# Attention inside a feed-forward sandwich: both layer norms of a batch in one ScalarE pass, whole-batch transfers in four pieces, V copied by VectorE, maxima placed either side of the scores

## The chip, the cores and the metric

One core of one Trainium2 chip runs the whole kernel. The metric is the device time in microseconds, the median of several runs; lower is better. Engines are named as in the profile: PE is TensorE (PEld its weight loads), DVE is VectorE, ACT is ScalarE, POOL is GpSimd, SP issues all DMAs.

## What is computed

Eight batches of 1024 tokens and 256 features go through half a mixture-of-experts feed-forward (`f1`), an attention (`at`), and the same feed-forward again (`f2`). Each stage gets a layer norm of its input, and the attention normalises once more inside:

```python
x = x + 0.5 * ffn(layernorm(x))
x = x + attention(layernorm(x))        # attention adds its own input as residual
x = x + 0.5 * ffn(layernorm(x))

def attention(x):                      # x is layernorm(x) already
    h = (x - mean) * rsqrt(var + 1e-5) * ln_scale + ln_bias
    c_q, c_kv = h @ w_down_q.T, h @ w_down_kv.T
    q, k, v = up-projections to 16 heads of 64; rotary embedding on q and k
    attn = softmax(q @ k.T / 8)
    return (attn @ v) @ w_out.T + x
```

So the residual of the attention stage is x + layernorm(x), and the down-projections read layernorm(layernorm(x)). The change touches the attention alone.

## The kernel before, in words

Three stages run one after the other: `ffn("f1")`, `attention`, `ffn("f2")`. In each, one list `order` of steps, written by rules, sets the order of every engine: `tensor`, `scalar`, `vector`, `gpsimd` and `sync` walk the same list and take the steps that concern them. Engines meet through semaphores only, and each works its own queue strictly in order.

The attention has NN = 64 "heads" n: step n is a pair of heads of one batch (8 batches, 8 pairs). A head has 8 **periods**, numbered 0 to 7 here. In a period PE does

- two score tiles (L827): for a key tile of 128 keys, 2 heads x 512 queries, three products with float32 values split in a high and a low part, added onto a PSUM buffer that ScalarE has *filled* beforehand with the negated row maxima (L913, from `SH`);
- two maxima matmuls for the next head (L806, step `most`), whose result VectorE reduces to row maxima (L988);
- two attend steps (L838): the exponentials `PT` times V;
- and, in `OT`, one or two of the small products: `raise` (q or k of the next head, L785), `value` (V, L797), `row` (the maxima transposed, L813), `sum` (L849), `outward` (the output projection, L862, at the odd heads' periods 0, 3 and 4), `turn` and `latent` (once per batch).

ScalarE does the exponentials (L922), the fills of the next period's two score tiles, and copies out of PSUM: `raise` (L890), `high` (L896, two per head, both in period 0), `value` (L901), `row`, `sum`, `attend`. VectorE does the two maxima reductions and then, late in the period, the rotary product (L971, reads PSUM), the rotation sum (L978, `rotate`, periods 4 to 7), `qlow` (L983), the residual addition (L1009), the sum of two row-sum halves (L997) and its reciprocal. GpSimd adds up the exponentials (L1053, `gather`), multiplies by the sines (L1032), divides, and makes `KL`.

The rows of maxima go over SP through memory: `row` is copied to `ML`, written to `MD` (L1081), and read back onto all partitions as `SH` (L1087, `shift`); ScalarE's fills wait for that.

Score tiles and maxima share a ring of three PSUM buffers, handed out in the order in which the steps stand: a use waits until the use three places earlier is read out.

```python
ring = Banks(3, [s for s in order if s[0] in ("score", "most")])
...
order += begin.get(g, []) + scores + mosts + early.get(g, []) + fills + attends
order += [("gather",) + s[1:] for s in attends if s[3] % 4] + late.get(g, []) + end.get(g, [])
```

At a batch boundary the batch `b + 2` is loaded by one 1 MB DMA (L1058), behind the store of batch b (L1114) for which it waits; both stand in SP's queue. In the next two heads the layer norms of the following batch run in two rounds r over 17 periods: 8 statistics (L948), 8 aggregates (L954) and 8 normalisations (L960, 128x256 each) on VectorE, the power -0.5 on GpSimd (L1020, L1022), and in the second round GpSimd's addition of the first norm onto X (L1026).

## Time and profile before

| | us |
|---|---|
| runs (3) | 4356.98, 4357.19, 4368.64; median 4357.19 |
| the profiled execution's own time | 4368.48 |
| its span | 4366.7 |
| PE busy | 4005.4 (92%) |
| ScalarE, GpSimd busy | 3010.3 (69%), 3049.4 (70%) |
| VectorE busy | 2756.6 (63%) |

Busy shares are means over three stages; the first exponential of the attention starts at 615 us, the last pair at 3800 us. Matmuls are pipelined and overlap in the records, so that PE's busy time is not PE at its peak. A timeline row merges like instructions that follow each other (xN).

### The profile page before, as it was taken

The numbers are of one execution on the slowest core, as the hardware profiler recorded it, in microseconds if no ns is written. First come the engines' busy times: TensorE is split into PE (matmuls) and PEld (weight loads), VectorE is DVE, ScalarE is ACT, GpSimd is POOL, SyncE is SP. The second block draws the span as 40 slices with busy tenths as digits, with TensorE's granted clock in tenths as the row PEclk, the third lists the DMA queues.
The fourth block names the chain that finished last, engine by engine and source line by source line (L and its number), as shares of the span: only waits on it lengthen the run. The fifth ranks groups of instructions, "written<-read, shape, count | busy, mean of one in ns | idle before, by whom it ended". The sixth has DMA issues, their size and how long they took to land. (4 is left out here: it accounts for less than half of the span.)

```text
span 4366.7 us, 65862 instructions
## 1 busy us (share of the span) xinstructions
PE 4005.4 (92%) x24896; PEld 2256.7 (52%) x24896; DVE 2756.6 (63%) x3555; ACT 3010.3 (69%) x3800; POOL 3049.4 (70%) x1597
## 2 busy tenths in 40 slices
PE   7999869999899989999998999899889999879999
PEld 6888724444344434444444444344444444358888
DVE  5556457656766675766667666766776667345653
ACT  4454348787778777877887787788777887735444
POOL 3444438878778787878887788788877887724444
PEclk9999979999999999999999999999999999979999
DMA  3333221111111211121112112111211121123332
GB/s 109 100 117 107 79 77 52 50 57 61 62 57 54 69 50 57 55 78 53 50 60 69 52 62 69 49 50 59 71 52 59 50 79 52 41 92 117 117 100 66
DMA packets 193645, 301.12 MB, mean 69 GB/s; under 512 B 50766, under 2 KB 101680, under 8 KB 192688
## 3 DMA queue, kind: packets, MB, share of 16 engines
q1 hardware_dynamic: 193328, 296.92, 21.2%
q8 instruction: 196, 3.21, 0.3%
q14 instruction: 121, 0.99, 0.1%
HBM read 201.92 MB, written 26.74 MB: 52 GB/s over the span
## 5 line engine op out<-in xcount | busy, mean ns | idle before, releaser
L988 DVE TENSOR_REDUCE atNM<-atPS 128x2 f32<-128x1024 f32 x1024 | 1205.9, 1220 | 804.0 <-PE atPS L806 801.4
L1053 POOL TENSOR_TENSOR atACC<-atACC,atPT 128x1024 f32<-128x1024 f32 x512 | 1285.1, 2510 | 63.0 <-ACT atPT L922 10.3
L922 ACT ACTIVATE atPT<-atPS 128x1024 f32<-128x1024 f32 x1024 | 995.7, 1023 | 201.7 <-PE atPS L827 195.1
L913 ACT ACTIVATE atPS<-atSH 128x1024 f32<-128x1024 f32 x1024 | 1009.5, 1022 | 87.1 <-DVE atNM L988 45.0
L838 PE MATMUL atPO<-atPT,atV 128*64 128x512 f32 x4096 | 974.3, 596 | 0.0
L1053 POOL TENSOR_TENSOR atACC<-atPT 128x1024 f32<-128x1024 f32 x256 | 624.0, 2437 | 105.3 <-PE atOT L849 103.7
L1032 POOL TENSOR_TENSOR atVT<-atVT,atSIN 128x512 f32<-128x512 f32 x256 | 342.8, 1339 | 366.6 <-DMA atVT<-atR 366.5
L806 PE MATMUL atPS<-atKH,atQH 64*128 64x512 f32 x2048 | 465.1, 455 | 121.0 <-ACT atPT L922 95.1
L838 PEld LDWEIGHTS atPO<-atPT,atV 128*64 128x64 f32 x4096 | 281.2, 137 | 477.1 <-issue 470.4
L827 PE MATMUL atPS<-atQH,atKL 64*128 64x512 f32 x2048 | 476.9, 462 | 45.2 <-ACT atPS L913 45.2
L827 PE MATMUL atPS<-atQH,atKH 64*128 64x512 f32 x2048 | 413.4, 399 | 0.0
L827 PE MATMUL atPS<-atQL,atKH 64*128 64x512 f32 x2048 | 412.7, 399 | 0.0
L827 PEld LDWEIGHTS atPS<-atQH,atKL 64*128 64x128 f32 x2048 | 195.1, 187 | 395.9 <-ACT atPS L913 208.5
L978 DVE TENSOR_TENSOR atU<-atU,atVT 128x512 f32<-128x512 f32 x256 | 393.0, 1535 | 3.4 <-POOL atVT L1032 3.4
L806 PEld LDWEIGHTS atPS<-atKH,atQH 64*128 64x128 f32 x2048 | 198.5, 189 | 368.1 <-ACT atPT L922 300.6
L506 POOL TENSOR_TENSOR f2GL<-f2GF,f2GH 128x512 fp32r<-128x512 f32 x144 | 199.6, 1389 | 257.8 <-ACT f2GH L354 253.1
L506 POOL TENSOR_TENSOR f1GL<-f1GF,f1GH 128x512 fp32r<-128x512 f32 x144 | 198.3, 1381 | 255.3 <-ACT f1GH L354 253.7
L890 ACT ACTIVATE atR<-atOT 128x512 f32<-128x512 f32 x256 | 153.1, 598 | 190.2 <-PE atOT L785 190.2
L862 PE MATMUL atOT<-atWO,atAT 128*64 128x256 f32 x2048 | 248.5, 385 | 19.2 <-POOL atAT L1038 13.4
L1038 POOL TENSOR_TENSOR atAT<-atAT,atRSUM 128x512 f32<-128x512 f32 x128 | 161.4, 1282 | 100.8 <-DMA atRSUM<-atRD 100.7
L827 PEld LDWEIGHTS atPS<-atQH,atKH 64*128 64x128 f32 x2048 | 197.9, 189 | 46.3
L862 PEld LDWEIGHTS atOT<-atWO,atAT 128*64 128x64 f32 x2048 | 143.7, 138 | 144.0 <-issue 41.4
(238 smaller groups left out, 6593.2 us busy)
## 6 DMA issues: line engine op xcount, KB each, us to landing
atVT<-atR SPq DMA_DIRECT2D x512, 128.0 KB, 2.0
atSH<-atMD SPq DMA_DIRECT2D x128, 512.0 KB, 4.4
f1GB<-f1GD SPq DMA_DIRECT2D x128, 256.0 KB, 6.8
atRSUM<-atRD SPq DMA_DIRECT2D x128, 256.0 KB, 4.0
f2GB<-f2GD SPq DMA_DIRECT2D x128, 256.0 KB, 6.9
x<-X SPq DMA_DIRECT2D x7, 1024.0 KB, 4.8
X<-x SPq DMA_DIRECT2D x7, 1024.0 KB, 5.4
f1XB<-in_x SPq DMA_DIRECT2D x5, 1024.0 KB, 5.3
```

The lines of the kernel that those rows point to most:

```text
L506: pool.eng.tensor_tensor(GL[n % NH][:, :], GF32[n % NH][:, :], GH[n % NH][:, :], ALU.subtract).then_inc(low_h.sem)
L806: ins = pe.eng.matmul(bank[:, h, :], QH[n % 2][HI[h], q * 128:(q + 1) * 128], KH[n % 2][HI[h], t * 512:(t + 1) * 512], start=True, stop=True)
L827: ins = pe.eng.matmul(bank[:, h, :], kk[HI[h], keys], q[HI[h], sl], start=False, stop=k == 2, skip_group_check=True)
L838: ins = pe.eng.matmul(PO[HI[h], :], V[n % 2][:, j, HI[h]], PT[k % NPT][:, h, :], start=j == 0, stop=j == T - 1)
L862: ins = pe.eng.matmul(OT[HI[c], i * D:(i + 1) * D], AT[:, (n - GP + 1 + q) % NAT, tok:tok + 64], WO[:, (p - GP + 1 + q) * D:(p - GP + 2 + ...
L913: act.eng.activation(PS[ring.of[("score", n, t, j)]][:, :, :], SH[t][:, :, :], ACT.Copy).then_inc(filled[j % 2].sem)
L922: act.eng.activation(PT[k % NPT][:, :, :], PS[ring.of[step]][:, :, :], ACT.Exp, scale=SCALE).then_inc(grown.sem)
L978: dve.eng.tensor_tensor(U[:, i, sl], U[:, i, sl], VT[k][:, :], ALU.add).then_inc(rotated.sem)
L988: dve.eng.tensor_reduce(NM[:, q // 4, :, q % 4, t], PS[ring.of[step]][:, :, :], AX.X, ALU.max, negate=True).then_inc(most_out.sem)
L1032: pool.eng.tensor_tensor(VT[k][:, :], VT[k][:, :], SIN[:, t * 512:(t + 1) * 512], ALU.mult).then_inc(sined.sem)
L1038: pool.eng.tensor_tensor(o, o, RSUM[n % 2][:, t * 512:(t + 1) * 512], ALU.mult).then_inc(divided.sem)
L1053: pool.eng.tensor_tensor(total[:, :, :], begun[:, :, :], PT[k % NPT][:, :, :], ALU.add).then_inc(gathered.sem)
```

## The change

In words, by steps:

- The list of a period becomes first maxima, two score tiles, second maxima, instead of scores, then both maxima.
- Step `value` (the copy of V out of PSUM) moves from ScalarE to VectorE, in the same place of the list.
- The row-sum halves are added by a reduction of one operand into a new `RI`, not by an addition of two.
- A batch's statistics are taken once, of X. GpSimd works out from mean and variance a scale and a bias for layernorm(layernorm(x)) and another pair for x + layernorm(x) (11 small dependent instructions); ScalarE applies both, 16 activations of 128x256 in four steps `norm`. The normalisations on VectorE, the second statistics and GpSimd's large addition go.
- Store and load of a batch become four DMAs of 256 KB each, each with its own semaphore and its own place in the list.

```diff
@@ the list @@
-                        again = [s and (s[0], b, r, s[1]) for r in range(2) for s in once()]
-                        for i, step in enumerate(again):
-                            at(end, m, -42 + i * 17 // len(again), *([step] if step else []))
+                        for i in range(4):
+                            at(end, m, -40 + i, ("stats", b, i))
+                            at(end, m, -33 + i, ("norm", b, i))
+                        at(end, m, -36, ("spread", b))
...
+                if p == NP - 1:
+                    for u, period in enumerate((25, 26, 28, 30)):
+                        at(end, m, period, ("store", b, u))
+                        if b + 2 < NB:
+                            at(end, m, period + 3 - u // 2, ("load", b + 2, u))
...
-                order += begin.get(g, []) + scores + mosts + early.get(g, []) + fills + attends
+                order += begin.get(g, []) + mosts[:1] + scores + mosts[1:] + early.get(g, []) + fills + attends
@@ scalar @@
+                    if name == "norm":
+                        _, b, i = step
+                        X = X0 if b == NB else XB[b % 2]
+                        act.wait_ge(*scales(b, 10 if b < NB else 3))
+                        act.wait_ge(*turned(b - 1, 1, 1))
+                        for k in (2 * i, 2 * i + 1):
+                            one, two = (slice(x * T + k, x * T + k + 1) for x in range(2))
+                            ins = act.eng.activation(Y[:, k, :], X[:, k, :], ACT.Identity, scale=A[:, two], bias=B[:, two])
+                            if b < NB:
+                                ins = act.eng.activation(X[:, k, :], X[:, k, :], ACT.Identity, scale=A[:, one], bias=B[:, one])
...
@@ vector @@
+                    elif name == "spread":
+                        _, b = step
+                        dve.wait_ge(*stats(b))
+                        dve.wait_ge(*scales.past(b - 1, 10))
...
+                    elif name == "value":
+                        _, n, t = step
+                        dve.wait_ge(*valued(n, t))
+                        dve.wait_ge(*attended.past(n - 2, 1, T - 1))
+                        dve.eng.tensor_copy(V[n % 2][:, 4 * t:4 * t + 4, :],
+                                            OT[:, :].rearrange("p (i d) -> p i d", d=128)).then_inc(value_out.sem)
...
-                        dve.eng.tensor_tensor(RQ[:, 0, :], RQ[:, 0, :], RQ[:, 1, :], ALU.add).then_inc(inverse.sem)
+                        dve.wait_ge(*lines.past(n - 1))
+                        dve.eng.tensor_reduce(RI[:, :], RQ[:, :, :].rearrange("p h i -> p i h"), AX.X, ALU.add,
+                                              negate=False).then_inc(inverse.sem)
@@ gpsimd, each of these waits for the one before @@
+                        then(0, pool.eng.tensor_scalar(RS[:, :], var, EPS, None, ALU.add))
+                        then(1, pool.eng.tensor_tensor(RS[:, :], RS[:, :], HALF[:, :], ALU.pow))
+                        then(2, pool.eng.tensor_scalar(NG[:, :], mean, -1.0, None, ALU.mult))
...
+                            then(8, pool.eng.tensor_tensor(A[:, two], A[:, two], HALF[:, :], ALU.pow))
+                            then(9, pool.eng.tensor_tensor(A[:, two], A[:, two], RS[:, :], ALU.mult))
+                            then(10, pool.eng.tensor_tensor(B[:, two], A[:, two], NG[:, :], ALU.mult))
@@ sync @@
-                def load(b):
-                    sp.wait_ge(*stored[b % 2].past(b - 2))
-                    sp.eng.dma_start(XB[b % 2][:, :, :], rows(src, b)).then_inc(loaded[b % 2].sem, 16)
+                def load(b, u):
+                    some = slice(2 * u, 2 * u + 2)
+                    sp.wait_ge(*stored[u].past(b - 2))
+                    sp.eng.dma_start(XB[b % 2][:, some, :], rows(src, b)[:, some, :]).then_inc(loaded[u].sem, 16)
```

PE, one period in the middle of a head (`atPS` with `atKH,atQH` alone are the maxima, L806 before and L817 now; L827 and L838 the scores). Before:

```order
L827 MATMUL atPS<-atQH,atKL 128x512 x2
L827 MATMUL atPS<-atQL,atKH 128x512 x2
L827 MATMUL atPS<-atQH,atKH 128x512 x2
L827 MATMUL atPS<-atQH,atKL 128x512 x2
L827 MATMUL atPS<-atQL,atKH 128x512 x2
L827 MATMUL atPS<-atQH,atKH 128x512 x2
L806 MATMUL atPS<-atKH,atQH 128x512 x4
L785 MATMUL atOT<-atCKV,atWK 64x512 x2
L838 MATMUL atPO<-atPT,atV 64x512 x4
```

Now:

```order
L817 MATMUL atPS<-atKH,atQH 128x512 x2
L838 MATMUL atPS<-atQH,atKL 128x512 x2
L838 MATMUL atPS<-atQL,atKH 128x512 x2
L838 MATMUL atPS<-atQH,atKH 128x512 x2
L838 MATMUL atPS<-atQH,atKL 128x512 x2
L838 MATMUL atPS<-atQL,atKH 128x512 x2
L838 MATMUL atPS<-atQH,atKH 128x512 x2
L817 MATMUL atPS<-atKH,atQH 128x512 x2
L796 MATMUL atOT<-atCKV,atWK 64x512 x2
L849 MATMUL atPO<-atPT,atV 64x512 x4
```

One of the two maxima matmul pairs has moved ahead of the scores. The ring of three now gives the second maxima the buffer of the same period's first.

VectorE, from period 4 of head 2 at a batch boundary. Before (L960 is a normalisation, L997 and L999 the row sums and their reciprocal, L993 the maxima's minimum):

```order
L971 TENSOR_TENSOR atU<-atOT,atCOS 128x512
L978 TENSOR_TENSOR atU<-atU,atVT 128x512
L997 TENSOR_TENSOR atRQ<-atRQ 128x16
L999 RECIPROCAL atRQ<-atRQ 128x16
L960 TENSOR_SCALAR Y<-X,atMV,atRS 128x256 x4
L993 TENSOR_REDUCE atMC<-atNM 128x8
L988 TENSOR_REDUCE atNM<-atPS 128x2 x2
L971 TENSOR_TENSOR atU<-atOT,atCOS 128x512
L978 TENSOR_TENSOR atU<-atU,atVT 128x512
L960 TENSOR_SCALAR Y<-X,atMV,atRS 128x256 x2
```

Now (L1001 are the maxima, L983 the copy of V, L991 the rotation):

```order
L978 TENSOR_TENSOR atU<-atOT,atCOS 128x512
L991 TENSOR_TENSOR atU<-atU,atVT 128x512
L1011 TENSOR_REDUCE atRI<-atRQ 128x16
L1014 RECIPROCAL atRI<-atRI 128x16
L969 BN_AGGR atMV<-atST 128x2 x8
L1006 TENSOR_REDUCE atMC<-atNM 128x8
L1001 TENSOR_REDUCE atNM<-atPS 128x2 x2
L978 TENSOR_TENSOR atU<-atOT,atCOS 128x512
L991 TENSOR_TENSOR atU<-atU,atVT 128x512
L1001 TENSOR_REDUCE atNM<-atPS 128x2 x2
L983 COPY atV<-atOT 128x512
```

The normalisations are gone from the queue, the aggregates stand where four of them stood, and the copy of V has come in behind a pair of maxima.

ScalarE, end of head 2 and head 3's first period, now (L939 exponentials, L930 fills, L919 the `high` copies, L888 and L890 the norm); before, the same stretch holds no L888 and L890:

```order
L939 ACTIVATE atPT<-atPS 128x1024 x2
L930 ACTIVATE atPS<-atSH 128x1024 x2
L888 ACTIVATE Y<-atXB,atB,atA 128x256
L890 ACTIVATE atXB<-atXB,atB,atA 128x256
L888 ACTIVATE Y<-atXB,atB,atA 128x256
L890 ACTIVATE atXB<-atXB,atB,atA 128x256
L939 ACTIVATE atPT<-atPS 128x1024 x2
L919 ACTIVATE atKH<-atU 128x1024
L930 ACTIVATE atPS<-atSH 128x1024 x2
L946 ACTIVATE atAT<-atPO 128x512
L919 ACTIVATE atQH<-atU 128x1024
L888 ACTIVATE Y<-atXB,atB,atA 128x256
```

Four activations come between the fills of one period and the exponentials of the next, in four periods on end.

## Rows read from the trace of the kernel before

**Rows 1.** The page: busy time, share of the span and instructions of each engine.

```profile
PE 4005.4 (92%) x24896; PEld 2256.7 (52%) x24896; DVE 2756.6 (63%) x3555; ACT 3010.3 (69%) x3800; POOL 3049.4 (70%) x1597
```

**Rows 2.** Windows of two heads: us, busy (x instructions), PEclk, DMA share, GB/s.

```profile
3435.10:3480.00 44.90, 42.23 (x261) 18.35 (x260) 31.63 (x30) 38.40 (x47) 39.53 (x20) 1.00 0.20 60
...
3480.00:3529.50 49.50, 47.95 (x324) 23.02 (x322) 33.36 (x34) 38.74 (x46) 40.42 (x20) 1.00 0.24 76
```

**Rows 3.** Timeline of one period, PE, VectorE, ScalarE: start, us, what [idle before].

```profile
1454.12 0.50 PE L827 MATMUL atPS<-atQH,atKL 64*128 64x512 f32 x2
...
1455.13 1.94 ACT L922 ACTIVATE atPT<-atPS 128x1024 f32<-128x1024 f32 x2 [0.27 <-PE atPS L827]
...
1455.62 0.39 PE L806 MATMUL atPS<-atKH,atQH 64*128 64x512 f32 x2
...
1456.05 1.23 DVE L988 TENSOR_REDUCE atNM<-atPS 128x2 f32<-128x1024 f32 x1 [1.85 <-PE atPS L806]
...
1456.20 0.51 PE L806 MATMUL atPS<-atKH,atQH 64*128 64x512 f32 x2 [0.20 <-ACT atPT L922]
```

**Rows 4.** Who waited for whom: us in total, times, longest us.

```profile
PE atPS L806 <- ACT atPT L922: 95.1, 449, 0.6
```

**Rows 5.** Timeline of ScalarE, period 0 of an even head: its two first exponentials.

```profile
1414.70 1.94 ACT L922 ACTIVATE atPT<-atPS 128x1024 f32<-128x1024 f32 x2 [0.39 <-PE atPS L827]
...
1420.79 1.94 ACT L922 ACTIVATE atPT<-atPS 128x1024 f32<-128x1024 f32 x2
```

**Rows 6.** Timeline of VectorE, end of period 4 into period 5, even head.

```profile
3462.19 2.60 DVE L978 TENSOR_TENSOR atU<-atU,atVT 128x512 f32<-128x512 f32 x1
...
3465.11 2.35 DVE L988 TENSOR_REDUCE atNM<-atPS 128x2 f32<-128x1024 f32 x2
```

**Rows 7.** Lines L978 and L971: duration ns min/median/max, first and last start, forms.

```profile
L978 DVE TENSOR_TENSOR atU<-atU,atVT x256: 674/1396/2918, 575.3 to 3722.0; 128x512 f32<-128x512 f32 x128
...
L971 DVE TENSOR_TENSOR atU<-atOT,atCOS x256: 673/692/693, 568.4 to 3710.4; 128x512 f32<-128x512 f32 x128
```

**Rows 8.** Windows: heads 1 to 3 of batch 7, sum of all eight batches'.

```profile
3480.00:3624.30 144.30, 138.49 (x904) 64.39 (x902) 99.20 (x104) 115.90 (x138) 121.38 (x58) 1.00 0.22 71
...
sum 1266.30, PE 1131.80 PEld 531.55 DVE 902.14 ACT 931.31 POOL 1002.47; mean PE 141.48 PEld 66.44 DVE 112.77 ACT 116.41 POOL 125.31
```

**Rows 9.** Timeline round a boundary, SP and ScalarE: load, row maxima out, fills.

```profile
1499.33 0.38 SPq L1058 DMA_DIRECT2D atXB<-x  x1
...
1507.51 0.52 SPq L1087 DMA_DIRECT2D atSH<-atMD  x1
...
1512.08 1.03 ACT L913 ACTIVATE atPS<-atSH 128x1024 f32<-128x1024 f32 x1 [5.45 <-DMA atSH<-atMD]
```

**Rows 10.** Timeline of head 2 at a boundary, VectorE and ScalarE.

```profile
1546.82 6.55 DVE L960 TENSOR_SCALAR Y<-atXB,atMV,atRS 128x256 f32<-128x256 f32 x4
...
1554.62 1.03 ACT L913 ACTIVATE atPS<-atSH 128x1024 f32<-128x1024 f32 x1 [6.71 <-DVE atNM L988]
```

**Rows 11.** Lines L876 and L890, ScalarE: duration ns min/median/max.

```profile
L876 ACT ACTIVATE atHT<-atOT,atlns x32: 762/777/784, 545.0 to 3337.3; 128x512 f32<-128x512 f32 x32
...
L890 ACT ACTIVATE atR<-atOT x256: 597/597/603, 567.7 to 3709.8; 128x512 f32<-128x512 f32 x128
```

**Rows 12.** Lines L1020, L1022 and L1026, GpSimd: duration ns min/median/max.

```profile
L1020 POOL TENSOR_SCALAR atRS<-atMV x15: 243/243/246, 716.9 to 3625.7; 128x8 f32<-128x8 f32 x15
...
L1022 POOL TENSOR_TENSOR atRS<-atRS,atHALF x15: 1665/1666/1667, 717.3 to 3626.0; 128x8 f32<-128x8 f32 x15
...
L1026 POOL TENSOR_TENSOR atXB<-atXB,Y x4: 4565/4566/4585, 770.6 to 3197.9; 128x2048 f32<-128x2048 f32 x4
```

**Rows 13.** Groups of instructions: busy us, mean ns | idle before, releaser.

```profile
L997 DVE TENSOR_TENSOR atRQ<-atRQ 128x16 f32<-128x16 f32 x64 | 40.7, 636 | 24.1 <-DMA atRQ<-atRSUM 24.1
...
L993 DVE TENSOR_REDUCE atMC<-atNM 128x8 f32<-128x16 f32 x128 | 18.4, 144 | 0.9
```

**Rows 14.** DMA issues: KB each, median us from issue to landing.

```profile
x<-atXB SPq DMA_DIRECT2D x4, 1024.0 KB, 4.7
```

More of the change, by code:

```diff
@@ L659, in attention @@
                         at(table, m, period, ("outward", m, u))
-            for i, step in enumerate([("next", 0), None, None] + [s and (s[0], NB, 0, s[1]) for s in once()]):
-                at(end, NN - 4, i, *([step] if step else []))
+                if p == NP - 1:
[3 more added lines that the diff above has]
+                            at(end, m, period + 3 - u // 2, ("load", b + 2, u))
+            at(end, NN - 4, 0, ("next", 0))
+            for i in range(4):
+                at(end, NN - 4, 3 + i, ("stats", NB, i))
+                at(end, NN - 4, 10 + i, ("norm", NB, i))
+            at(end, NN - 4, 7, ("spread", NB))
             order = []
@@ L996, in vector @@
                         dve.wait_ge(*columns(n))
-                        dve.eng.tensor_tensor(RQ[:, 0, :], RQ[:, 0, :], RQ[:, 1, :], ALU.add).then_inc(inverse.sem)
+                        dve.wait_ge(*lines.past(n - 1))
+                        dve.eng.tensor_reduce(RI[:, :], RQ[:, :, :].rearrange("p h i -> p i h"), AX.X, ALU.add,
+                                              negate=False).then_inc(inverse.sem)
                         dve.wait_ge(inverse.sem, inverse(n)[1] - 1)
-                        dve.eng.reciprocal(RQ[:, 0, :], RQ[:, 0, :]).then_inc(inverse.sem)
+                        dve.eng.reciprocal(RI[:, :], RI[:, :]).then_inc(inverse.sem)
                     elif name == "outward":
@@ new lines, in gpsimd, with then @@
+                        one, two = slice(0, T), slice(T, 2 * T)
+                        mean, var = MV[:, :, 0], MV[:, :, 1]
+                        def then(k, ins):
+                            ins.then_inc(scales.sem)
+                            pool.wait_ge(*scales(b, k))
+                        pool.wait_ge(*means(b))
+                        pool.wait_ge(*normed.past(b - 1))
+                        last = two if b == NB else one
+                        then(0, pool.eng.tensor_scalar(RS[:, :], var, EPS, None, ALU.add))
@@ L1065, in sync @@
                     sp.eng.dma_start(x[:, :], a[name]).then_inc(outs.sem, 16)
-                load(1)
+                for u in range(4):
+                    load(1, u)
                 for step in order:
```

111 lines of the change are left out of this document (48 added, 63 removed).

## The prediction

> **What bounds the kernel now.** The page first: of the span PE is busy 92%, the four others between 52% and 70% [rows 1]; an average over two feed-forward stages and the attention. So I cut the attention into heads by the starts of the exponentials (L922) and asked for the busy time of each stretch. Two undisturbed heads, an even one and an odd one (the odd one carries the output projection), take 44.9 and 49.5 us [rows 2]. PE is busy 42.2 and 48.0 of them at full granted clock, ScalarE 38, GpSimd 40, VectorE 32 to 33: PE first, nobody far behind. Inside a head the eight periods, as distances between first exponentials, are 6.1, 5.5, 6.2, 5.2, 5.5, 5.6, 6.2 and 4.4 us (even; the first is the distance between the two rows of [rows 5]) and 7.8, 5.5, 6.2, 7.0, 7.0, 5.5, 6.2, 4.4 (odd), the same to 0.02 us wherever no batch boundary lies.
>
> In the timeline of one period [rows 3] the reader is to see that the scores start at 0, the first pair of maxima matmuls at 1.50, the second not 0.23 later but at 2.08: it needs the PSUM buffer that the first exponential empties. That wait appears 449 times [rows 4]. This is the 0.35 us that the reorder is aimed at; 512 periods make 179 us.
>
> Batch boundaries are the second loss. Heads 1 to 3 of a batch (counted from 0) carry the store and load of whole batches and both layer norms. Eight such triples take 1266.3 us; the last batch's, which has neither, takes 144.3 [rows 8], the first batch's has one projection less (139.7 if undisturbed). 1266.3 - 7 x 144.3 - 139.7 = 116.5 us are lost there; a further 4.5 go to the last norm, in head 4 of the last batch. Two causes are visible. The load waits in the SP queue for the whole store, and what is issued behind it lands late: ScalarE idles 5.45 us for the row maxima [rows 9]. And norm instructions of 0.32 us take 2.5 each on VectorE while GpSimd works, so four of them hold the queue 6.55 us and ScalarE waits 6.71 for a maximum behind them [rows 10].
>
> **The change, part by part.** (0 is the first matmul of a period.)
>
> *Maxima either side of the scores.* Removed: the wait for the exponential. Added: with three PSUM buffers the second maxima now need the buffer of the first, so PE waits for VectorE in the same period. If VectorE is free, its reduction starts 0.43 after the matmul (1456.05 against 1455.62), takes 1.22, and the second maxima go at 1.70 instead of 2.08; the scores before them end their issue at 1.61. A bare period falls from 4.39 to about 4.0 by PE; ScalarE's chain (two exponentials, two fills at a pitch of 0.92 to 0.96, 0.35 from fill to exponential) allows about 4.15. Gain 0.25 to 0.4. But whatever VectorE still has from the period before now stands ahead of a reduction that PE waits for; before, it had until 1.93. The rotations (L978, both inputs in SBUF) take 0.67 to 2.92, median 1.40, four per head; the PSUM-fed product beside them 0.69 always [rows 7]. I walked both heads through with 1.5 us per rotation and 2.0 for L983. Even head: period 1 goes to 4.1 (-1.4: PE no longer waits for an exponential that the two 1.05 us copies hold back, and the copy of V leaves ScalarE), periods 3, 4 and 7 gain 0.5, 0.6 and 0.45, period 5 loses 0.7, because product, rotation and reciprocal end 1.9 us into it, the last ones of [rows 6]; the others move 0.1 either way: -2.3. Odd head: 3, 4 and 7 gain 0.9 together, but at period 4 the residual addition waits for the projection and the rotation stands behind it, so the maxima of period 5 come 2.3 late: +1.9 there; with 0.1 won in 1 and 2 that is +0.9. Sum: 32 x (-2.3 + 0.9) = **-45 us**. What is late next is VectorE's queue at period 5.
>
> *V copied by VectorE, the reciprocal's sum as a reduction.* Both are within that walk. The copy has no row; the nearest are the PSUM-fed product, 0.69, and the norms at up to 2.6. I take 0.69, as both move 512 columns out of PSUM. ScalarE loses 0.60 twice a head. The sum of two halves (L997) averages 0.64 with both inputs in SBUF, a small reduction 0.14 [rows 13]; I take 0.14. SBUF — State Buffer of the Trainium skill (Who interferes with whom) says that a VectorE instruction with two SBUF inputs, or in a 2-port mode, is locked out by a GpSimd one that reads SBUF, and that a tensor_reduce never is. By that rule both prices hold; without it they are 0.64 and up to 2.6, and the sum is up to 31 us (0.48 x 64) worse for the one and some 60 (half of 128 copies exposed by 1) for the other.
>
> *One pass of norm on ScalarE.* VectorE loses per batch 8 statistics, 8 aggregates and 16 normalisations, and with them the 6.55 us blocks. ScalarE gets 16 activations of 256 columns with per-partition scale and bias, in four steps of four at periods 7, 0, 1, 2. A 512-column one with both takes 0.777, a plain one 0.597 [rows 11]; at 0.83 us per thousand columns (1.02 for 1024) 256 columns are 0.56, at a pitch of 0.49. Bounds: 0.39 (plain) to 0.78. So 2.0 us per step: +1.9 in period 7, +0.4 in period 0 (odd, PE has slack), +0.7 and +1.0 after: 4.1 x 7 = +29. Statistics and aggregates stay on VectorE, at the ends of periods 0 to 3 and 4, ahead of maxima that PE waits for: +1.5 x 7 = +10. GpSimd loses two pows and the 4.57 addition and gets a chain of 11 dependent ones, two of them pows of 1.67, nine like the addition of 0.24: 6.2 us with the hand-overs, against two rounds of both and one addition of 4.57 before [rows 12], but all of it at period 4, its fullest, ahead of the sine products that rotations need; the queue, which in a head of 45 us is busy 40 [rows 2], falls behind by about 7.4 with the wait for the aggregates, of which some 3.7 is slack before a rotation asks: 3.7 late, +26. The final norm keeps half of its cost, +2.
>
> *Transfers in pieces.* The load of a piece now waits for a store issued two to three periods earlier, which has landed, so the SP queue no longer stops; 256 KB instead of 1 MB stand ahead of the small transfers. Cover for the loads: the statistics come four periods later, some 20 us. Left over 0.5 x 7 = +3.5. At the end the stage waits for the last store, 4.7 us for 1 MB [rows 14]; it becomes 256 KB. Bounds 0 and 3.5 (a quarter of the time); I take **-2.5**.
>
> Boundaries: -117 - 4 + 29 + 10 + 26 + 2 + 3.5 = **-50.5**. Sum: -45 - 50.5 - 2.5 = -98 us. The profiled execution took 4368.5 (span 4366.7 and 1.8 around it) and would take 4270; it lies 11.3 above the median of the three runs, 4357.2, for which the same sum gives **4259**. The forecast's own bounds: 4215 to 4300.
>
> **The rivals.**
> *Maxima wait for VectorE (slower).* The place is the first reduction of periods 0, 2, 5 and 7, behind rotations. In rows rotations of 2.6 are common [rows 6]. Three of four per head are exposed; each 0.1 us over my 1.5 costs 0.1 x 3 x 64 = 19 us. From 2.0 on the change loses (98 / 192 = 0.51 over); at 2.2 the time is 4259 + 0.7 x 192 = 4393. For it: the new wait ties GpSimd, VectorE and PE in one loop. Against: VectorE has 13 us or more free in a head [rows 2], and GpSimd no more work than before. Chance 0.10.
> *The reorder gives all.* If rotations fall where GpSimd is idle, 0.38 is won in seven of eight periods: 448 x 0.38 = 170 instead of 45: 4134. For: the even head alone shows it; against: the odd one. Chance 0.15.
> *Only one half pays.* Either the new wait eats the reorder (0, then 4304), or the GpSimd chain and ScalarE's extra 8 us put the boundary stalls back (about 0 there, then 4310). Chance 0.25.
> *The change does not do what it says*: a stall only moves and nothing is measurable: 4357, chance 0.05. Against it stands that the load's stop in SP's queue is plain [rows 9].
> The forecast has 0.45.
>
> **How the numbers follow.** A difference under 0.3% (13 us; 4344 to 4370) cannot be told from none. Faster: 0.45 + 0.15 + 0.25 = 0.85; within: 0.05; slower: 0.10. The predicted time is the likeliest case's, 4259. The range leaves out the slow rival (0.10) and the outer ends: from the full gain of the reorder, 4134, with a little for a boundary that costs less than I charge, 4125, to 4345, which takes in the half-paid cases and V copies that are locked out.
>
> **What would show it.** The distance from the first maxima matmul to the second should be 1.7 in a free period and up to 4 in period 5, its releaser the reduction, no longer L922's exponential; the undisturbed heads 42 to 43 and 50 to 51 us; GpSimd idle before its sines only at the boundaries; no ScalarE wait over 3 us for the row-maxima transfer; the triple of heads at a boundary near 152 instead of 164; activations of the norm 0.56 each; V copies 0.69 and never 2.5. I am wrong if the odd head falls under 48.5 or rises over 52, if V copies vary in length, or if the triples stay above 158.

## The result: 0.6% slower, outside the forecast's range

| | before | changed |
|---|---|---|
| median of 6 runs each, same chip | 4362.91 us | 4390.67 us |
| ratio, 95% interval | | 1.0061 [1.004, 1.0082] |
| boundary triples (heads 1 to 3), sum | 1266.3 | 1233.9 |
| the other 39 heads | 1882.2 | 1948.5 |

The forecast was 4259 (4125 to 4345). The two lower rows are from the profiled executions. The triples and the other heads part ways: the boundaries gained, the steady state lost twice that. (The 39 are the heads 0 and 4 to 7 of each batch, up to the last head but one.)

The page of the changed kernel, busy time of the engines, beside [rows 1]:

```profile
span 4394.0 us, 65989 instructions
...
PE 3959.9 (90%) x24896; PEld 2280.5 (52%) x24896; DVE 2688.6 (61%) x3451; ACT 3012.1 (69%) x3792; POOL 3035.3 (69%) x1642
```

PE is busy for 45 us less in a span that is longer: it waits. Windows of an even and an odd undisturbed head (columns as in [rows 2]), then of the last batch's triple and the sum of the eight [rows 8]:

```profile
1426.88:1474.84 47.96, 42.16 (x260) 19.68 (x260) 31.34 (x32) 37.80 (x45) 40.15 (x20) 0.96 0.18 56
1376.40:1426.88 50.48, 47.84 (x324) 23.32 (x324) 32.41 (x36) 37.99 (x44) 39.87 (x20) 1.00 0.18 54
...
3502.80:3654.89 152.09, 139.47 (x904) 67.36 (x904) 98.03 (x109) 113.79 (x133) 120.67 (x58) 0.98 0.21 67
sum 1233.88, PE 1101.89 PEld 526.86 DVE 814.13 ACT 959.82 POOL 988.17; mean PE 137.74 PEld 65.86 DVE 101.77 ACT 119.98 POOL 123.52
```

The even head was to fall to 42 to 43 us and went from 44.9 to 48; the odd one, at 50 to 51, is where it was forecast. Even the last triple, which has neither norm nor load, is 7.8 longer. By period, medians of the distances between first exponentials (heads 0 and 7 of batches 1 to 6, as all period medians below; the distance called k runs from period k's first exponential to the next period's, so a stop at the start of period 1 lengthens distance 0):

| period | 0 | 1 | 2 | 3 | 4 | 5 | 6 | 7 |
|---|---|---|---|---|---|---|---|---|
| even, before | 6.09 | 5.48 | 6.23 | 5.24 | 5.51 | 5.64 | 6.25 | 4.40 |
| even, changed | 8.49 | 5.62 | 6.77 | 4.98 | 5.00 | 5.51 | 7.31 | 4.13 |
| odd, before | 7.84 | 5.46 | 6.24 | 6.97 | 6.96 | 5.45 | 6.25 | 4.39 |
| odd, changed | 7.70 | 5.38 | 5.97 | 6.71 | 6.88 | 6.37 | 7.31 | 4.12 |

So the gain is there in periods 3, 4 and 7, at the low end of the 0.25 to 0.4 that was forecast, and is lost in periods 0 and 2 of the even heads, in 6, and in the odd heads' 5. Who waits for whom from 700 to 3700 us (us in total, times, longest):

```profile
PEld atPS L817 <- DVE atNM L1001: 337.3, 422, 2.5
...
PE atPS L817 <- DVE atNM L1001: 163.1, 148, 2.1
PE atPS L817 <- ACT atQH L919: 87.0, 30, 3.4
```

Before, the exponentials ended the maxima's waits [rows 4]. Now it is VectorE's reduction, as meant, but up to 2.5 us; and a row stands there that the prediction has no word on: the maxima (L817) wait for `high`, L919. All 30 stand at the start of an even head's period 1; the timeline of one:

```profile
1427.94 1.94 PE L849 MATMUL atPO<-atPT,atV 128*64 128x512 f32 x8
...
1431.58 0.58 ACT L946 ACTIVATE atAT<-atPO 128x512 f32<-128x512 f32 x1
1432.06 1.05 ACT L919 ACTIVATE atQH<-atU 128x1024 fp32r<-128x1024 f32 x1
...
1433.25 0.80 PE L817 MATMUL atPS<-atKH,atQH 64*128 64x512 f32 x2 [3.37 <-ACT atQH L919]
...
1433.82 0.66 PE L838 MATMUL atPS<-atQH,atKL 64*128 64x512 f32 x2
```

The first maxima of the next head need its `QH`, ScalarE's last copy of period 0. Before, they stood behind the two score tiles, which do not need it; now they stop PE's queue 3.37 us. The pairs then take 0.80 and 0.66 where 0.50 and 0.39 are usual. Windows of PE over the stop and behind it:

```profile
1429.90:1433.20 3.30, 0.00 (x0) 1.00 0.00 0
1433.20:1436.30 3.10, 3.05 (x14) 0.50 0.03 5
```

After 3.3 us without a matmul the clock is granted at 0.50, the lower of its two levels (1.2 GHz), for 3.1 us; this happens behind some of the stops, not all. Odd heads cover the copy with their outward projection: none of the 30 waits is theirs. The other large loss, in period 6 of another even head:

```profile
1866.03 0.69 DVE L978 TENSOR_TENSOR atU<-atOT,atCOS 128x512 f32<-128x512 f32 x1 [0.42 <-ACT atR L913]
...
1866.22 5.15 POOL L1084 TENSOR_TENSOR atACC<-atACC,atPT 128x1024 f32<-128x1024 f32 x2
1866.64 2.52 DVE L991 TENSOR_TENSOR atU<-atU,atVT 128x512 f32<-128x512 f32 x1
...
1867.20 0.50 PE L817 MATMUL atPS<-atKH,atQH 64*128 64x512 f32 x2
...
1869.08 1.21 DVE L1001 TENSOR_REDUCE atNM<-atPS 128x2 f32<-128x1024 f32 x1
...
1870.35 0.50 PE L817 MATMUL atPS<-atKH,atQH 64*128 64x512 f32 x2 [1.27 <-DVE atNM L1001]
```

The first maxima are done at 1867.7, but VectorE's reduction starts at 1869.08, behind a rotation of 2.52, and the second maxima come 3.15 after the first. The first of GpSimd's two additions ended at 1868.61; the rotation ended 0.55 later. In the odd heads' period 5 the queue is long without that (head 7 of batch 2):

```profile
1813.07 0.69 DVE L1024 TENSOR_TENSOR X<-X,atOT 128x512 f32<-128x512 f32 x1 [2.12 <-PE atOT L873]
1813.67 0.68 DVE L991 TENSOR_TENSOR atU<-atU,atVT 128x512 f32<-128x512 f32 x1
...
1814.68 1.22 DVE L1001 TENSOR_REDUCE atNM<-atPS 128x2 f32<-128x1024 f32 x1
...
1815.96 0.50 PE L817 MATMUL atPS<-atKH,atQH 64*128 64x512 f32 x2 [1.13 <-DVE atNM L1001]
```

The rotation is short there, but it stands behind a residual addition that waits for the projection, and three small instructions follow it.

### The profile page after: what moved, and what is told of

Same layout as the page of the kernel before. It is cut to its first block and busy times, and to the rows that moved or that the text cites. A ratio compares the mean times of both kernels' runs of the same rounds, so it can differ in the third digit from the quotient of the medians.

```text
span 4394.0 us, 65989 instructions
## 1 busy us (share of the span) xinstructions
PE 3959.9 (90%) x24896; PEld 2280.5 (52%) x24896; DVE 2688.6 (61%) x3451; ACT 3012.1 (69%) x3792; POOL 3035.3 (69%) x1642
## 5 line engine op out<-in xcount | busy, mean ns | idle before, releaser
L1001 DVE TENSOR_REDUCE atNM<-atPS 128x2 f32<-128x1024 f32 x1024 | 1252.8, 1224 | 768.1 <-PE atPS L817 766.5
L939 ACT ACTIVATE atPT<-atPS 128x1024 f32<-128x1024 f32 x1024 | 995.7, 1022 | 328.7 <-PE atPS L838 321.5
L930 ACT ACTIVATE atPS<-atSH 128x1024 f32<-128x1024 f32 x1024 | 1013.5, 1022 | 77.0 <-DVE atNM L1001 43.6
L817 PE MATMUL atPS<-atKH,atQH 64*128 64x512 f32 x2048 | 513.4, 498 | 287.5 <-DVE atNM L1001 173.1
L1084 POOL TENSOR_TENSOR atACC<-atPT 128x1024 f32<-128x1024 f32 x256 | 637.7, 2491 | 172.4 <-PE atOT L860 162.8
L817 PEld LDWEIGHTS atPS<-atKH,atQH 64*128 64x128 f32 x2048 | 198.0, 188 | 750.6 <-issue 359.9
L1063 POOL TENSOR_TENSOR atVT<-atVT,atSIN 128x512 f32<-128x512 f32 x256 | 328.9, 1285 | 285.0 <-DMA atVT<-atR 284.9
L838 PE MATMUL atPS<-atQH,atKL 64*128 64x512 f32 x2048 | 423.5, 405 | 18.5 <-ACT atPS L930 18.5
L838 PE MATMUL atPS<-atQH,atKH 64*128 64x512 f32 x2048 | 418.3, 399 | 0.0
L838 PE MATMUL atPS<-atQL,atKH 64*128 64x512 f32 x2048 | 417.7, 399 | 0.0
L991 DVE TENSOR_TENSOR atU<-atU,atVT 128x512 f32<-128x512 f32 x256 | 361.7, 1413 | 15.2 <-POOL atVT L1063 15.2
L978 DVE TENSOR_TENSOR atU<-atOT,atCOS 128x512 f32<-128x512 f32 x256 | 177.1, 692 | 148.4 <-ACT atR L913 148.4
L838 PEld LDWEIGHTS atPS<-atQH,atKL 64*128 64x128 f32 x2048 | 201.7, 190 | 73.4 <-ACT atPS L930 53.7
L838 PEld LDWEIGHTS atPS<-atQH,atKH 64*128 64x128 f32 x2048 | 203.0, 190 | 41.7
```

The lines of the kernel that those rows point to most:

```text
L817: ins = pe.eng.matmul(bank[:, h, :], QH[n % 2][HI[h], q * 128:(q + 1) * 128], KH[n % 2][HI[h], t * 512:(t + 1) * 512], start=True, stop=True)
L838: ins = pe.eng.matmul(bank[:, h, :], kk[HI[h], keys], q[HI[h], sl], start=False, stop=k == 2, skip_group_check=True)
L930: act.eng.activation(PS[ring.of[("score", n, t, j)]][:, :, :], SH[t][:, :, :], ACT.Copy).then_inc(filled[j % 2].sem)
L939: act.eng.activation(PT[k % NPT][:, :, :], PS[ring.of[step]][:, :, :], ACT.Exp, scale=SCALE).then_inc(grown.sem)
L978: dve.eng.tensor_tensor(U[:, i, sl], OT[:, :], COS[:, sl], ALU.mult).then_inc(cosine.sem)
L991: dve.eng.tensor_tensor(U[:, i, sl], U[:, i, sl], VT[k][:, :], ALU.add).then_inc(rotated.sem)
```

## Experiments

Every kernel was timed beside the kernel before on the same chip (its medians 4357.0, 4366.9, 4363.5, 4365.2 and 4359.3 in the five groups of runs), so differences between kernels are told by the ratios; 0.001 is 4.4 us. A ratio's 95% interval is some 0.002 to either side, so a difference of two ratios is good to 10 to 15 us. "Old order" is scores before both maxima, "new order" the change's.

### The parts apart

**Old order, rest of the change.**

```diff
-order += begin.get(g, []) + mosts[:1] + scores + mosts[1:] + ...
+order += begin.get(g, []) + scores + mosts + ...
```

> The changed kernel with the maxima back behind the scores; norm on ScalarE, pieces and V on VectorE stay. Theory (the new order is what costs: PE waits for the copy of the next head's Q at period 1 of the even heads, and for VectorE's reductions at periods 5 and 6; the rest of the change pays at the boundaries): 4290, between 4275 and 4305, clean heads 44 to 45 and 49 to 50 us. Rival (the parts moved onto VectorE and ScalarE cost as much as the order): 4330 or more, clean heads over 46 and 50.

4292.4, ratio 0.9842 [0.9818, 0.9866], as expected: 69 us faster than before; the undisturbed heads are those of before to 0.1 us, the triples 1203.4. So the rest of the change gives 69 and the new order takes 95 (0.0219) away. TensorE's mean granted clock from 700 to 3700 us was 0.98 before, 0.99 in the changed kernel and 1.00 here, so a part of the gain is the clock, no longer lowered at the boundaries; how much was not taken apart.

**New order alone**, the same line in the kernel before.

> The kernel before with the new order alone. Theory: the even heads lose about 3 us and the odd ones 0.9, as in the changed kernel: +100 to +125, 4460 to 4490. Rival (the order costs only together with the V copy on VectorE): under 4400.

4522.3, ratio 1.0373 [1.0348, 1.0397]: dearer still, and more than expected. Even heads' period 5 takes 9.2 us (median).

**V copied by ScalarE again**, old order:

> As the first one (maxima behind the scores), and the copy of V back on ScalarE: what is left are the norm on ScalarE, the pieces and the reduction of the row sums. Theory: V costs 0.60 on ScalarE twice a head where PE sets the pace, so within 10 us of the first one, 4280 to 4305. Rival (ScalarE is close enough to PE that V there costs): 4310 or more.

4306.6, 0.9881 [0.9857, 0.9904]: just outside what was expected. V on VectorE is worth 17 us by the ratios, barely more than their noise; the profiled executions have 9 of it in the triples and 2 in the 39 other heads. **The kernel before with V on VectorE and nothing else:**

> The kernel before with the V copy on VectorE and nothing else. The old order with whole transfers (4308) differs from this one by the norms and the row sums alone. Theory (V gives some 10 us at the boundaries, the norms 30 to 50): 4340 to 4357. Rival (with the norms still on VectorE its queue at a boundary gets longer by the copies, and V costs there): 4360 or more.

4382.6, 1.0037 [1.0023, 1.0051]: the rival. With the norms on VectorE the copies cost 16 us, and the triples are 17 longer (1283.6). That VectorE's queue is full there is the likely reason; no run takes it apart.

**Transfers together again**, old order (eight transfers at period 28, stores first):

```diff
-for u, period in enumerate((25, 26, 28, 30)):
-    at(end, m, period, ("store", b, u))
-    if b + 2 < NB: at(end, m, period + 3 - u // 2, ("load", b + 2, u))
+for u in range(4): at(end, m, 28, ("store", b, u))
+for u in range(4):
+    if b + 2 < NB: at(end, m, 28, ("load", b + 2, u))
```

> The old order of a period and the rest of the change, but the four stores of a batch stand together behind the last outward product, with the four loads of the next but one batch right behind them in SP's queue, as the whole-batch transfers stood before. Theory (the loads' wait for the stores stops SP's queue and the row maxima land late): head 1's period 7 takes some 3.7 us more (9.64 before against 5.98 with pieces), six or seven times, with a little more behind it: 4310 to 4335. Rival (the pieces did nothing, the boundary's gain is the norms' alone): 4300 or less.

4307.8, 0.9869 [0.9849, 0.9888], 12 us above the old order with spread pieces (the triples 19, 1222.7), a little under what was expected: head 1's period 7 takes 8.36 (5.98 spread, 9.64 before). Between this kernel and the one with nothing but V on VectorE lie the norms and the row sums: 0.0168, 73 us.

### Where the new order loses

**Period 1 old, the others new.**

```diff
+ahead = 0 if g % PER == 1 else 1
-... + mosts[:1] + scores + mosts[1:] + ...
+... + mosts[:ahead] + scores + mosts[ahead:] + ...
```

> The changed kernel, but in period 1 of each head both maxima stand behind the scores as before; all other periods keep the new order. Theory (first maxima of a head need the copy of its Q, which ScalarE makes last in period 0, and the scores queue behind them): period 0 to 1 of the even heads falls from 7.6-8.5 to about 6.1, 32 x 1.5 to 2.4: 4310 to 4345. Rival (only waits for VectorE behind rotations cost, as my slow rival said): within 10 us of the changed kernel, 4380 or more.

4378.4, 1.0039 [1.0019, 1.0058], neither. Period 0 of even heads healed (8.49 to 6.13), but period 2 of odd ones went from 5.97 to 8.06: the loss moved on. **New order in chosen periods only** (3, 4, 7; 5, 6; 1), old elsewhere:

> The change, with the new order of a period kept only in periods 3, 4 and 7; in the others the maxima stand behind the scores again. Theory (the new order gains where the first maxima matmul finds its operand and VectorE ready, and loses in periods 1, 5 and 6): the clean heads of the change had periods 3, 4, 7 at 4.98, 5.00, 4.13 (even) and 6.71, 6.88, 4.12 (odd) where the old order has 5.24, 5.51, 4.40 and 6.97, 6.96, 4.39: 1.04 less in an even and 0.61 less in an odd head, 53 us in 64 heads below the 4292 of the run with the old order: 4240. Rival (each new-order period pushes its loss into the next one, as putting period 1 back did, so that the gain can't be had apart): 4290 or more.

> The change, with the new order kept only in periods 5 and 6. Theory (in those periods PE waits for VectorE's reductions, which stand behind rotations, residual additions and sums): even heads 0.13 less in period 5 and 1.06 more in period 6, odd heads 0.92 and 1.06 more; 93 us in all above the 4292 of the old order: about 4385, and at least 4350. Rival (the loss comes from somewhere else, from the order at the head's start alone): 4300 or less.

> The change, with the new order kept only in period 1. Theory (in an even head the first maxima matmul of period 1 needs the high copy of the next head's Q, ScalarE's last instruction of period 0, and now stops PE's queue ahead of the scores): period 0 of even heads goes from 6.1 to 7.8 or more, the odd ones hide the copy behind their outward products; 32 even heads by 1.5 to 2.4 us: 4340 to 4370. Rival (the copy is covered when nothing else is late): 4300 or less.

| new order in | median | ratio [95%] | beside the old order |
|---|---|---|---|
| 3, 4, 7 | 4264.1 | 0.9763 [0.975, 0.9776] | -34 |
| 5, 6 | 4405.6 | 1.0085 [1.0072, 1.0099] | +106 |
| 1 | 4343.4 | 0.9944 [0.993, 0.9957] | +44 |

All three signs and the last two sizes are as the theory has them; of the 53 expected for 3, 4, 7 two thirds came. So beside the old order the wait for the `high` copy alone costs 44, and periods 5 and 6 alone cost 106. The three add up to 116 and not to 95: what a period does depends on its neighbours' order.

The 44 are two costs. In the run with period 1 alone, head 0 of batches 1 and 2, periods 0 and 1 (us, busy, PEclk, DMA share, GB/s):

```profile
1008.91:1021.46 12.55, 9.45 (x67) 4.95 (x65) 7.64 (x8) 10.28 (x12) 12.12 (x6) 1.00 0.00 0
1406.31:1420.19 13.88, 10.78 (x67) 6.11 (x65) 8.40 (x8) 10.39 (x13) 13.31 (x7) 0.88 0.01 1
```

The old order has 11.56 (6.09 + 5.47). Of its even heads from 2 to 62, 16 kept the full clock and lost 0.99 (median) in these two periods; in 15 the clock was granted at 0.50 for a part of them, and they lost 2.32. The wait costs 1 us, the lowered clock another 1.3 in about half of the even heads: some 19 of the 50 us that these heads lose in this trace.

In the run with periods 5 and 6 alone an even head's period 5 takes 9.0 us. VectorE and GpSimd there:

```profile
1857.66 2.75 DVE L992 TENSOR_TENSOR atU<-atU,atVT 128x512 f32<-128x512 f32 x1
1860.34 0.17 DVE L1012 TENSOR_REDUCE atRI<-atRQ 128x16 f32<-128x32 f32 x1
...
1860.74 1.22 DVE L1002 TENSOR_REDUCE atNM<-atPS 128x2 f32<-128x1024 f32 x1
...
1857.46 2.40 POOL L1085 TENSOR_TENSOR atACC<-atPT 128x1024 f32<-128x1024 f32 x1
...
1862.02 0.79 PE L818 MATMUL atPS<-atKH,atQH 64*128 64x512 f32 x2 [2.25 <-DVE atNM L1002]
```

Again the rotation ends (1860.41) 0.55 after GpSimd's addition (1859.86). This rotation, late in period 4, lasts 2.60 to 2.75 here in head 0 of batches 1 to 6 and 0.92 to 0.95 in the changed kernel, where GpSimd is at a short sine product instead; the matmuls behind the wait run at half the clock (0.79 for the pair). So 106 is not what the two periods cost in the change: its own medians give 32 x (1.06 - 0.13 + 0.92 + 1.06) = 93.

**3, 4, and 7 in odd heads only:**

> The change, with the new order kept in periods 3 and 4 of every head and in period 7 of the odd heads only. Theory (a period's place decides: in the run with 3, 4 and 7 the even heads' periods 6 and 7 took 6.48 + 4.97 against 6.25 + 4.40 with the old order, the odd ones' 6.48 + 3.93 against 6.24 + 4.38; 3 and 4 gain in both): 32 even heads by 0.8 us less than that run, 26 us: about 4240 beside a kernel before of 4367. Rival (the even heads' loss comes in with periods 3 and 4 and stays): no difference from that run's 4264.

4266.4, 0.9772 [0.9751, 0.9793]: the rival, no difference from 3, 4, 7. **Rotations behind the next period's first maxima:**

> The change, with each rotation that stood at a period's end moved behind the first maxima of the next period, so that VectorE does the first reduction of periods 5, 6, 7 and 0 ahead of it. Theory (PE waits in periods 5 and 6 for reductions that stand behind rotations): period 6 falls from 7.3 to about 6.0 and the odd period 5 from 6.4 to about 5.5, some 70 us less: 4300 to 4345. Rival (the rotation is only passed on, now it stands ahead of the second reduction, or it isn't what delays the reduction): 4385 or more.

4420.9, 1.012 [1.0103, 1.0137], the rival. Period 6 of even heads did fall, 7.31 to 5.99, but the loss came back one period later, 4.12 to 5.73 (even) and 6.26 (odd), and elsewhere.

### Is a rotation long, or held?

**Rotations of 64 columns** in place of 512, with the new and with the old order:

```diff
-dve.eng.tensor_tensor(U[:, i, sl], U[:, i, sl], VT[k][:, :], ALU.add)
+few = slice(t * 512, t * 512 + 64)
+dve.eng.tensor_tensor(U[:, i, few], U[:, i, few], VT[k][:, :64], ALU.add)
```

The other columns of the rotary sum are left out.

> The change whole, but each rotation on VectorE adds 64 of its 512 columns only, so that it takes some 0.1 to 0.3 us in place of 0.7 to 2.5; this leaves part of the rotary embedding out. Theory (in periods 5 and 6 PE waits for maxima reductions behind rotations): even heads' period 6 from 7.3 to about 6, odd heads' periods 5 and 6 from 6.4 and 7.3 to 5.4 and 6: some 100 us off the 4391 of the change, 4280 to 4310; what is left above the old order is the wait for the high copy. Rival (rotations are not what delays PE; the reductions wait for PE's own order or for GpSimd): 4350 or more.

> The same short rotations with the old order of a period, the rest of the change kept. Theory (in the old order a scores' time stands between the reduction and the next use, so the rotation is covered): within 20 us of the 4292 of the old order with whole rotations, and within 30 us of the change with short ones, where the two orders are 98 apart with whole ones. Rival (VectorE binds both orders alike, the short rotation helps both): 60 us or more below 4292.

4337.9, 0.9941 [0.9924, 0.9958], and 4276.1, 0.98 [0.978, 0.982]: half of the gain expected of the first (52 us); the second gained 18, within the 20 expected, and the two orders still stand 62 apart, where 30 was the most expected. The timeline of the first tells why. Period 6 again:

```profile
1835.00 4.89 POOL L1085 TENSOR_TENSOR atACC<-atACC,atPT 128x1024 f32<-128x1024 f32 x2
1835.52 1.95 DVE L992 TENSOR_TENSOR atU<-atU,atVT 128x64 f32<-128x64 f32 x1
...
1837.39 1.21 DVE L1002 TENSOR_REDUCE atNM<-atPS 128x2 f32<-128x1024 f32 x1
...
1838.66 0.50 PE L817 MATMUL atPS<-atKH,atQH 64*128 64x512 f32 x2 [0.69 <-DVE atNM L1002]
```

An eighth of the columns, and 1.95 us. Its first addition ends at 1837.38, the rotation at 1837.47. Over the whole trace: of the 256 rotations of the changed kernel 214 overlap a GpSimd instruction that ends before them (an addition, a sine product or a division), and end 0.54 to 0.62 after it; those of 64 columns 0.08 to 0.15 after. That is a little less than the time they take alone (0.68 and 0.22, the medians of the other 42). A rotation's duration is the wait for GpSimd, then its work.

**One operand in place of two**, 32 columns, as the row sums have it, with new order, old order, and period 1 old:

```diff
+few = slice(t * 512, t * 512 + 16)
+dve.eng.tensor_reduce(U[:, i, few], VT[k][:, :32].rearrange("p (h i) -> p i h", i=16), AX.X, ALU.add, negate=False)
```

> The change whole, but in the rotation's place VectorE runs a reduction of one operand of 32 columns, as the row sums do; this leaves the rotary sum out. Theory (a rotation with two SBUF inputs is held until GpSimd's addition ends, whatever its size, and the maxima reduction behind it keeps PE waiting): the rotation's 1.9 to 2.5 us in periods 4 and 5 become under 0.3, even heads' period 6 falls from 7.3 to about 6.0, the odd ones' 5 and 6 to 5.4 and 6.0: 4290 to 4330, below the 4338 of the 64-column rotations. Rival (VectorE's queue is late for other reasons, the V copies and products above all): 4335 or more.

> The old order of a period and the rest of the change with the same one-operand instruction in the rotation's place. Theory (the old order covers the rotation): 4260 to 4290, within 15 us of the 4276 with 64-column rotations. Rival (the hold costs the old order too): below 4255.

> The change with period 1 in the old order and the one-operand instruction in the rotation's place: both waits that were seen are gone. Theory (what was forecast of the new order, some 45 us, is there once nothing keeps its first maxima waiting): 20 to 60 us below the old order with the same instruction, 4215 to 4260. Rival (the loss moves on again, as it did when period 1 alone was put back): 4280 or more.

| | median | ratio [95%] |
|---|---|---|
| new order | 4258.3 | 0.9758 [0.9733, 0.9783] |
| old order | 4274.5 | 0.9789 [0.9764, 0.9814] |
| new, period 1 old | 4268.9 | 0.978 [0.9755, 0.9804] |

The new order is 132 us below the change, more than expected. The old order gains 23, as expected. The same place in the timeline:

```profile
1801.36 4.92 POOL L1086 TENSOR_TENSOR atACC<-atACC,atPT 128x1024 f32<-128x1024 f32 x2
...
1802.17 0.18 DVE L992 TENSOR_REDUCE atU<-atVT 128x16 f32<-128x32 f32 x1
...
1803.27 1.23 DVE L1003 TENSOR_REDUCE atNM<-atPS 128x2 f32<-128x1024 f32 x1 [0.93 <-PE atPS L817]
...
1804.55 0.49 PE L817 MATMUL atPS<-atKH,atQH 64*128 64x512 f32 x2
```

VectorE now waits for PE; period 6 is 5.99. Period 5 of the odd heads is 5.86, down from 6.37 by the 0.5 that the shorter rotation saves, and 0.4 above the old order: that loss is the queue's length and not a held instruction. The three kinds of rotation in the view of one line (duration ns min/median/max; change, 64 columns, one operand):

```profile
L991 DVE TENSOR_TENSOR atU<-atU,atVT x256: 675/1079/2927, 573.4 to 3751.6; 128x512 f32<-128x512 f32 x128
```

```profile
L992 DVE TENSOR_TENSOR atU<-atU,atVT x256: 210/615/2482, 564.2 to 3695.1; 128x64 f32<-128x64 f32 x128
```

```profile
L992 DVE TENSOR_REDUCE atU<-atVT x256: 174/177/190, 566.0 to 3611.1; 128x16 f32<-128x32 f32 x128
```

The third kernel, at 4269, lies between theory and rival: with period 1 old, period 2 rose to 7.75 (even) and 6.48 (odd) where 5.97 is free. There `qlow`, the other instruction with two SBUF inputs, then stands ahead of a reduction. Its mean was 2.58 us in that kernel. **`qlow` with one operand too:**

```diff
-dve.eng.tensor_tensor(QL[n % 2][:, :], U[:, 0, :], QH[n % 2][:, :], ALU.subtract)
+dve.eng.tensor_reduce(QL[n % 2][:, :], SIN[:, :].rearrange("p (i h) -> p i h", h=1), AX.X, ALU.add, negate=False)
```

> As the run with period 1 in the old order and a one-operand instruction for the rotation, and qlow is a reduction of one operand too (1024 columns of the sine table, so that its size stays; this leaves the low part of Q out). Theory (both two-operand instructions are held by GpSimd, and with neither in the way and the high copy waited for behind the scores the new order gives what was forecast): period 2 falls from 7.75 (even) and 6.48 (odd) to about 6.0, 4190 to 4230, some 45 to 80 below the old order with the short instruction (4274). Rival (something else of VectorE's queue, the number of its instructions, keeps period 2 long): 4255 or more.

4181.3, 0.959 [0.9565, 0.9615]: below even the expected range. An even and an odd head of it:

```profile
1356.24:1399.86 43.62, 41.32 (x260) 18.40 (x260) 25.53 (x32) 37.59 (x45) 37.97 (x20) 1.00 0.20 62
1307.61:1356.24 48.63, 47.70 (x324) 23.16 (x324) 28.01 (x36) 37.98 (x44) 38.48 (x20) 1.00 0.17 56
```

Period 2 is 5.97 in both. Beside the old order with the short rotation the new one now gives 87 us (0.0199). The old order with `qlow` shortened was not run, so a part of the 87 may be `qlow`'s alone. Against more than a small part: in the old order the undisturbed heads' period 2 is 6.24, as in the kernel before. Only in heads 5 and 6 of a batch is it 6.5, wherever V is on VectorE; 0.3 x 16 = 5 us could be won there. The gain lies in all heads: the undisturbed ones take 43.0 and 48.6 against 44.6 and 49.5, and the medians of a batch's eight heads are 10.1 lower together, 81 over the eight batches.

### A version that beats both

**Norm activations in eight steps of two** (periods -31 to -25 and -23 of the batch), new order in 3, 4 and the odd 7:

```diff
-for i in range(4): at(end, m, -33 + i, ("norm", b, i))
+for k, period in enumerate((-31, -30, -29, -28, -27, -26, -25, -23)):
+    at(end, m, period, ("norm", b, k))
```

> The new order in periods 3 and 4 and the odd heads' 7, and the 16 norm activations of a batch in eight steps of two, one in each of eight periods that have no high copies, in place of four steps of four. Theory (a step of 2.1 us delays the exponentials by 1.2 to 1.6 us in each of four periods, 40 us in seven boundaries, since ScalarE has some 1 us to spare in a period): half or more of the 40 goes, 4230 to 4250. Rival (ScalarE has nothing to spare there, work is only spread): 4260 or more.

4252.7, 0.975 [0.9729, 0.9771], the lowest of those that compute everything: 2.5% below before. The triples fell by 11.5 to 1176.0, but beside 0.9772 the intervals overlap, and it lies between theory and rival: in head 3 a smaller step still costs 0.3 to 0.8 us in most periods.

## Why the prediction was wrong

*The reorder, -45 us: the step that failed.* It gave +95 beside the old order. Most of the miss is in the even heads: heads 0 and 4 of a batch take 3.0 and 3.4 us more (head 6 0.35), where -2.3 was forecast. Step by step:

- The wait for the exponential went, as said. In a free period the second maxima come 1.82 after the first (1802.73 and 1804.55 in the run with one operand) and not 1.70: the reduction starts 0.54 behind the matmuls, not 0.43. Periods 3 and 7 gain 0.26 and 0.27 in an even head, not 0.5 and 0.45; the prediction's own bound for a bare period (ScalarE's 4.15 against 4.39) allowed 0.25, and the walk went past it. Period 4 gained 0.51 of 0.6.
- "Period 1 goes to 4.1 (-1.4)": it takes 5.2 where the clock stays full and 5.4 to 7.0 where it was lowered, after 5.5. Why it is not 4.1 at full clock stays open.
- "The others move 0.1 either way" is where most was lost. It held no look at what the *first* maxima of a period need. In period 1 that is the next head's `high` copy: +44 us, shown by the run with that period alone, some 40% of it by the clock, which the prediction does not price. The wait was in the trace of before, 23 times from 700 to 3700 us and never over 0.6 us, because the scores stood ahead of it (the view of who waits for whom, kernel before):

```profile
PE atPS L806 <- ACT atQH L896: 12.5, 23, 0.6
```

- The walk took every rotation at 1.5 us, near the median of [rows 7]. The changed kernel's mean is 1.41: the price was right and of no use. A held rotation has no length of its own: it ends 0.55 after GpSimd's instruction. Late in period 5 it is issued just as the first of two additions has begun and lasts over 2 us in 49 of 62 heads, ahead of period 6's first reduction; late in periods 4, 6 and 7 it mostly lasts 0.7 to 1.1. Period 6, "0.1", lost 1.06 in both heads, and the run with one operand gave it back. Period 5 lost 0.92 of the 1.9 forecast in the odd head, by the queue that was forecast (residual addition, rotation, small instructions) and a rotation of 0.68, and nothing of 0.7 in the even one. So the odd head came out at 50 to 51 by luck: two errors cancel.
- `qlow` had 2.0 in the walk and is the same case: in the run with one-operand rotations and period 1 old its mean was 2.58, ahead of a reduction, and period 2 took 7.75; with one operand for `qlow` too it is 5.97.

The page SBUF — State Buffer of the Trainium skill says it in so many words (Summary: rules for kernel authors): where VectorE has two SBUF inputs and GpSimd reads SBUF, the second to issue "fully blocks" until the first one is done. The runs with 64 columns and with one operand agree, 1.95 against 0.18 us. The prediction used that rule to price the row sum and the V copy, and not for the rotations, of which its own paragraph before says "both inputs in SBUF".

*V copies and row sums.* Right: copies 679/681/693 ns, never held; the row sum 0.18 against 0.14. Below, the copy of V and, for the next paragraph, a norm activation:

```profile
L983 DVE COPY atV<-atOT x128: 679/681/693, 588.7 to 3788.4; 128x512 f32<-128x512 f32 x128
```

```profile
L888 ACT ACTIVATE Y<-atXB,atB,atA x32: 584/588/592, 757.3 to 3218.2; 128x256 f32<-128x256 f32 x32
```

*Boundaries, -50.5.* Right in sign and near in size: the old-order run is 69 below before (with the tail's -2.5, which was not tested apart, 53 were forecast). The forecast had V's copy in the walk; with it back on ScalarE the run is 52 below, a hit by luck too, since terms are off both ways. They are: a norm activation is 0.588, not 0.56, and the four steps cost 1.5, 0.8, 1.2 and 1.6 (medians of heads 2 and 3 there: 5.91, 8.61, 6.68, 7.80 against 4.40, 7.85, 5.46, 6.23) and not 1.9, 0.4, 0.7 and 1.0: 35 against 29. With 1203.4 - 7 x 144.6 - 139.7 = 51.5 left in all, statistics, GpSimd's chain and transfers together cost 16, where 10, 26 and 3.5 were charged. The transfers are most of it: head 1's period 7 is at 5.98, 1.6 x 7 = 11, and there ScalarE's fills wait 1.5 to 2.5 us for the row maxima. In the old-order run head 2's periods 0 to 6, where the statistics and the chain stand, are those of an undisturbed head but for 0.6 to 0.9 in three places, so both charges were too high, 26 for the chain most of all. Two slips of reading change nothing in the sum: the four norm instructions of [rows 10] took 0.32, 1.49, 2.42 and 2.56, not 2.5 each, and the four costs of the norm steps add up to 4.0, not 4.1. In the changed kernel itself the new order takes 30 of this gain back, 1233.9 against 1203.4.

*The rivals.* "Maxima wait for VectorE" had 4393 and the change took 4391. Its mechanism is half of it: the wait is there, in the periods behind rotations. But its condition, a mean rotation of over 2.0, was not met (1.41), and `high` is no part of it. That the time agrees is luck. A chance of 0.10 was too low: the unnamed condition was not how long rotations are but when they are issued. "The reorder gives all" is what the run with one-operand rotation and `qlow` shows in part, 87 of 170, and needs two instructions that are not held. "Only one half pays" has the right half, but let the reorder fall to 0 at worst. None of the three signs of being wrong showed: the odd head is at 50.4, the V copies don't vary, the triples are at 155. None of them watched the start of the even head.

## What to carry to other kernels

When a step is put ahead of others in an in-order queue, list what each moved instruction needs and when that is ready at *every* place in the loop, above all where a new item begins: here a wait of 0.6 us at most behind independent work became one of 3.4 us ahead of it. Don't price an instruction by its mean if its duration holds a wait for another engine: look when it is issued against that engine's long instructions, and where the operation allows, give instructions on a tight loop one operand. To find such a wait, shrink the instruction: if an eighth of the size still takes most of the time (1.95 us here, of 2.5), it is being held.

## What was not expected of the hardware

- A rotation of 64 columns takes up to 2.48 us (median 0.62), one of 512 up to 2.93 (median 1.08).
- The same copy of V, 0.68 us on VectorE, makes the triples 9 us shorter where the norms are on ScalarE and 17 longer where they are on VectorE.
- The 3.4 us stop in front of period 1 was followed by 3.1 us at half the clock, in which 14 matmuls passed. With period 1 alone in the new order, heads whose clock stayed full lost 0.99 us in periods 0 and 1, those whose clock was lowered 2.32.
